# Layer 2 of a two-layer recurrent kernel: query and key norms together, keys kept in their bank, decay means moved to the tail, chunk sums in quarters

## The reference

```python
xn = layer_norm(x, ln1_w, ln1_b)
q, k, v = heads(xn @ Wq), heads(xn @ Wk), heads(xn @ Wv)
q = l2_normalize(q);  k = l2_normalize(k)
alpha = sigmoid(xn @ Wg + bg)
log_a   = log(maximum(alpha, 1e-6))
la_cum  = cumsum(log_a, within a chunk)
la_mean = la_cum.mean(-1)
decay   = exp(la_mean[:, None] - la_mean[None, :]) * tril
o_intra = ((q @ k.T) * decay) @ v
kv_chunk = (k * exp(la_cum[-1] - la_cum)).T @ v
chunk_decay = exp(log_a.sum())
q_dec = q * exp(la_cum)
# scan over the four chunks: o = q_dec @ S ; S = S * chunk_decay + kv_chunk
x = x + (o_intra + o_inter) @ Wo
x = x + gelu(layer_norm(x) @ W1 + b1) @ W2 + b2
```

## Time and profile before

| what | value |
|---|---|
| median of three executions | 2235.43 us (2231.66 to 2240.91) |
| the profiled execution, its own time | 2234.39 us |
| its span in the trace | 2232.6 us |
| TensorE busy | 1934.6 us, 87% |
| VectorE busy | 1362.9 us, 61% |
| ScalarE busy | 1096.1 us, 49% |
| mean granted TensorE clock | 0.953 of full |

### The profile page before, as it was taken

The page is one execution under the profiler, slowest core; times in us unless marked ns, Lnnn a source line. Parts: engine busy times, 40 slices in busy tenths (PEclk is TensorE's granted clock), DMA queues, the critical chain, the costliest instruction groups (busy, mean ns, idle before and its releaser), DMA issues.

```text
span 2232.6 us, 50773 instructions
## 1 busy us (share of the span) xinstructions
PE 1934.6 (87%) x17956; PEld 1381.8 (62%) x17972; DVE 1362.9 (61%) x3678; ACT 1096.1 (49%) x2434; POOL 214.6 (10%) x235
## 2 busy tenths in 40 slices
PE   6999999998999999959888988898988899898652
PEld 4666666666666666636667566765766676666552
DVE  6666666666666666637665765577666566755312
ACT  3444444443555445425665465555555554555332
POOL 0000000000000000030011001101111110010022
PEclk9999999999999999969999999999999999999887
DMA  3222222222122211230221112110211111111374
GB/s 127 79 87 87 87 87 92 91 86 64 59 68 68 67 49 53 75 116 23 63 67 47 56 56 66 52 30 24 67 46 58 58 53 41 37 46 42 124 233 119
DMA packets 97041, 159.05 MB, mean 71 GB/s; under 512 B 14279, under 2 KB 65607, under 8 KB 93640
## 3 DMA queue, kind: packets, MB, share of 16 engines
q1 hardware_dynamic: 87720, 134.93, 18.7%
q0 software_dynamic: 9248, 23.17, 3.4%
HBM read 96.35 MB, written 61.69 MB: 71 GB/s over the span
## 4 chain that ended last, share of the span: by engine, by line
PE 59%; DVE 20%; ACT 7%; issue 7%; SPq 3%; DMA 2%; POOL 1%; another core or an unknown queue 1%; DVEq 0%; ACTq 0%; POOLq 0%
PE psum L1032 5%; PE psum L870 5%; PE psum L937 4%; PE psum L830 4%; PE psum L764 3%; PE psum L1012 3%; PE psum L987 3%; PE psum L1142 3%; PE psum L952 2%; PE psum L1090 2%; PE psum L959 2%; PE psum L786 2%; PE psum L904 2%; PE psum L1041 2%; PE psum L877 2%
## 5 line engine op out<-in xcount | busy, mean ns | idle before, releaser
L1349 ACT ACTIVATE pts<-psum 128x512 f32<-128x512 f32 x192 | 99.1, 603 | 201.1 <-PE psum L904 201.1
L1803 DVE TENSOR_REDUCE mneg<-psum 128x2 f32<-128x512 f32 (+1 forms) x192 | 119.1, 683 | 46.8 <-PE psum L885 25.1
L671 POOL DMA_INDIRECT rows<-h,recA x64 | 61.5, 961 | 894.7 <-DVE recA L1585 767.3
L786 PE MATMUL psum<-txT,wt 128*128 128x128 f32 x864 | 118.9, 281 | 32.1 <-ACT txT L1241 32.0
L786 PEld LDWEIGHTS psum<-txT,wt 128*128 128x128 f32 x864 | 106.7, 194 | 43.9 <-ACT txT L1241 38.4
L870 PE MATMUL psum<-wa,xT_s 128*128 128x512 f32 x256 | 118.0, 603 | 2.6 <-DVE mneg L1803 2.6
L1032 PE MATMUL psum<-xT_s,wa 128*128 128x256 f32 x512 | 116.6, 381 | 0.0
L695 POOL DMA_INDIRECT rows<-xn,recC x32 | 31.5, 983 | 861.5 <-DVE recC L2007 741.3
L1550 DVE TENSOR_TENSOR tg<-tg,psum 128x256 f32<-128x256 f32 x84 | 35.2, 419 | 113.6 <-ACT tg L1230 109.2
L1032 PEld LDWEIGHTS psum<-xT_s,wa 128*128 128x128 f32 x512 | 95.8, 192 | 12.9 <-issue 1.0
L795 PE MATMUL psum<-wt,tg 128*128 128x128 f32 x528 | 79.2, 280 | 14.6 <-DVE tg L1552 13.8
(11 more groups left out here) (272 smaller groups left out, 4862.7 us busy)
## 6 DMA issues: line engine op xcount, KB each, us to landing
wt<-in_wB SPq DMA_DIRECT2D x84, 384.0 KB, 2.9
outs<-pbd SPq DMA_DIRECT2D x16, 1024.0 KB, 7.2
wt<-in_wD SPq DMA_DIRECT2D x24, 578.0 KB, 3.5
wa<-in_wD SPq DMA_DIRECT2D x15, 578.0 KB, 3.6
tx<-rows SPq DMA_DIRECT2D x132, 64.0 KB, 2.9
outs<-ty SPq DMA_DIRECT2D x132, 64.0 KB, 1.6
rows<-pbd SPq DMA_DIRECT2D x64, 128.0 KB, 1.7
rows<-pbd SPq DMA_DIRECT2D x8, 1024.0 KB, 3.9
```

Source lines behind the costliest of these rows:

```text
L786: last = mm(bank(f"th{j}")[:, c * P:(c + 1) * P], view[s][:, c * P:(c + 1) * P], txT[:, s, :], start=True, stop=True)
L1349: af(pT[:, n, :], bank(f"e{n}"), ACT.Exp, scale=float(HD) ** -0.5).then_inc(*frees(f"e{n}"))
L1803: ins = v.tensor_reduce(mneg[:, int(n >= 4), col:col + hs], sc, AX.X, ALU.max, negate=True)
```

## The change

Six edits, all in the P and C stages.

1. **Norms.** The squared queries and the squared keys are summed per head by a 128x32 matrix `headsum` into one bank `nq` (32 rows per group of four heads: queries in columns 0 to 255, keys in 256 to 511). One clamp, one logarithm and one exponential serve both. The query norms are spread to 64 rows by `headrow` (banks `rb`), the key norms are turned to token order (`rkT`).
2. **Keys.** The second projection of the keys is gone: `tk` is now 16 transposes of `kT`, and VectorE multiplies the decay with the bank directly. The copy, the squares in token order and their reduction go.
3. **Key projection.** `lk` moves from the tail of the previous turn to the head of C, between `te` and tile step 0.
4. **Decay means.** The logarithm (`decays`, ScalarE) and the means and their spreading (`decay_means`, VectorE) move from the head of C to the tail of the turn before; the clamps (L1686) move ahead of `wo1`. TensorE's first work in C is now `d`.
5. **Quarters.** `d`, `te` and `la` are computed in 64x64 pieces, one for each half of rows and half of columns. For that the second half of the heads has its two chunks swapped in `z` (`chunk_rows`).
6. **Bias of z.** `ones3` and `bg3` are kept in four row groups; the four bias products are issued together, ahead of the wait for the turned inputs. At the program's start that takes 4 loads of `ones3` in place of 1 and 12 small DMAs for `bg3` in place of 3, and ScalarE, VectorE and TensorE wait for 192 on `bg3_ready` in place of 48.

The core of the diff, SyncE's loads and TensorE:

```diff
+        def chunk_rows(half, ch):
+            r = ch ^ half
+            return slice(r * CH, (r + 1) * CH)
...
-            load(ones3[:, :], A["ones3"])
+            for g in range(4):
+                load(ones3[32 * g:32 * g + 3, :], A["ones3"])
...
             for i in range(3):
-                sp.dma_start(bg3[i:i + 1, :], kd_b16(i)).then_inc(sem("bg3_ready"), 16)
+                for g in range(4):
+                    sp.dma_start(bg3[32 * g + i:32 * g + i + 1, :], kd_b16(i)).then_inc(sem("bg3_ready"), 16)
...
-            def z_products(t):
+            def z_products():
+                places = [(t, c) for t in range(NT) for c in range(2)]
+                for g, (t, c) in enumerate(places):
+                    pe.wait_ge(*emptied(f"z{t}{c}"))
+                    mm(bank(f"z{t}{c}"), ones3[32 * g:32 * g + 3, :], bg3[32 * g:32 * g + 3, c * 512:(c + 1) * 512], start=True, stop=False)
+                pe.wait_ge(*read_out("zT"))
+                for t in range(NT):
+                    mm(bank(f"z{t}0"), xT[:, 1, t * P:(t + 1) * P], lqkvg[:, 3 * INNER:3 * INNER + 512], start=False, stop=True).then_inc(*fills(f"z{t}0"))
+                    pe.sem_inc(sem("tiles_open"), 1)
+                    for ch in range(2):
+                        place = chunk_rows(1, ch)
+                        last = mm(bank(f"z{t}1")[place, :], xT[:, 1, t * P + ch * CH:t * P + (ch + 1) * CH], lqkvg[:, 3 * INNER + 512:4 * INNER], start=False, stop=True)
+                    last.then_inc(*fills(f"z{t}1"))
...
             def attention1():
                 zT = xT[:, 1, :]
+                pe.wait_ge(*given("at3_ready", 0))
+                quads = [(hh, ch) for hh in range(2) for ch in range(2)]
+                for t in range(NT):
+                    for hh in range(2):
+                        pe.wait_ge(*emptied(f"d{t}{hh}"))
+                        mm(bank(f"d{t}{hh}"), identb[:, :], dmask[:, :, :], start=True, stop=False)
+                    pe.sem_inc(sem("tiles_open"), 1)
+                    for hh, ch in quads:
+                        rows = chunk_rows(hh, ch)
+                        last = mm(bank(f"d{t}{hh}")[ch * CH:(ch + 1) * CH, :], strict[rows, rows], at3[rows, t, 8 * hh:8 * hh + 8, :], start=False, stop=True)
...
+                    for hh, ch in quads:
+                        rows = chunk_rows(hh, ch)
+                        last = mm(bank(f"te{t}{hh}")[ch * CH:(ch + 1) * CH, :], strict[rows, rows], a_tok[rows, t, hh * 512:(hh + 1) * 512], start=True, stop=True)
...
+                products("lk", INNER)
+                tile_step(0)
                 pe.wait_ge(*given("sq_done", 0))
+                pe.wait_ge(*given("sk_done", 4))
                 for j in range(4):
-                    pe.wait_ge(*emptied(f"nq{j}"))
+                    pe.wait_ge(*read_out(f"lk{j}"))
+                pe.wait_ge(*emptied("nq"))
+                pe.sem_inc(sem("tiles_open"), 1)
+                for i, squares in enumerate((sqT, sqK)):
                     for a in range(2):
-                        last = mm(bank(f"nq{j}")[:, a * N:(a + 1) * N], samehead[:, :], sqT[:, 2 * j + a, :], start=True, stop=True)
-                    last.then_inc(*fills(f"nq{j}"))
-                for t in range(NT):
-                    for c in range(2):
-                        pe.wait_ge(*emptied(f"tk{t}{c}"))
-                        mm(bank(f"tk{t}{c}"), zT[:, t * P:(t + 1) * P], lqkvg[:, INNER + c * 512:INNER + (c + 1) * 512],
-                           start=True, stop=True).then_inc(*fills(f"tk{t}{c}"))
-                tile_step(0)
+                        for j in range(4):
+                            last = mm(bank("nq")[32 * j:32 * j + 32, i * N:(i + 1) * N], headsum[:, a, :], squares[:, 2 * j + a, :], start=(a == 0), stop=(a == 1))
+                last.then_inc(*fills("nq"))
                 tile_step(1)
...
+                for t in range(NT):
+                    last = tr(bank("rkT")[:, t * P:(t + 1) * P], rqk[:, 1, t * P:(t + 1) * P])
+                last.then_inc(*fills("rkT"))
+                for j in range(4):
+                    pe.wait_ge(*emptied(f"rb{j}"))
+                pe.sem_inc(sem("tiles_open"), 1)
+                for a in range(2):
+                    for j in range(4):
+                        rows = slice(32 * j, 32 * j + 32)
+                        last = mm(bank(f"rb{j}")[:, a * N:(a + 1) * N], headrow[rows, a, :], rqk[rows, 0, :], start=True, stop=True)
...
+                for t in range(NT):
+                    for c in range(2):
+                        pe.wait_ge(*emptied(f"tk{t}{c}"))
+                        for a in range(4):
+                            last = tr(bank(f"tk{t}{c}")[:, a * P:(a + 1) * P], kT[:, 4 * c + a, t * P:(t + 1) * P])
```

ScalarE at the head of C (after the decay exponentials), and VectorE's tail:

```diff
+                for j in range(4):
+                    act.wait_ge(*filled(f"lk{j}"))
+                    src = bank(f"lk{j}").rearrange("p (a n) -> p a n", a=2)
+                    af(sqK[:, 2 * j:2 * j + 2, :], src, ACT.Square).then_inc(*signals("sk_done"))
+                    af(kT[:, 2 * j:2 * j + 2, :], src, ACT.Copy).then_inc(*frees(f"lk{j}"))
+                tile_step(0)
+                first_gate()
+                act.wait_ge(*read_out("nq"))
+                af(rqk, rqk, ACT.Ln, scale=1e6).then_inc(*signals("act_chain"))
+                act.wait_ge(*chained("act_chain"))
+                af(rqk, rqk, ACT.Exp, scale=-0.5).then_inc(*signals("rq_ready"))
...
+                clamps()
                 dve.wait_ge(*filled("wo1"))
...
-                clamps()
+                decay_means(0)
+                decay_means(1)
                 tile_step(5)
```

235 lines of the change are left out of this document (114 added, 121 removed).

## The result

| | before | after |
|---|---|---|
| median, same chip | 2238.74 us (2231.66 to 2240.91, 6 runs) | 2255.92 us (2253.01 to 2265.38, 6 runs) |
| profiled execution | 2234.39 us | 2257.25 us |
| its span | 2232.6 us | 2255.5 us |
| TensorE busy | 1934.6 us | 1860.7 us |
| TensorE's matmul records | 17956 | 20500 |

The changed kernel takes 1.0089 times the time of before, 95% interval 1.0070 to 1.0108: 0.9% slower. 2200 us was forecast, and 2256 lies outside the range of 2150 to 2250.

What follows compares the result with a forecast made beforehand. TensorE's list was the main bound, VectorE holding it at certain places. B turns 33, D turns and CP 25, CD 0.6 gave -58.5; one-time costs +3.4 and +7, clock +13: net -35, 2200 us, range 2150 to 2250.

Steps and rivals of the forecast that it cites:

- Price of the quarters: Four 64x64 quarter products over 512 columns on TensorE were taken at 1.0 us, with ends of 0.86 and 3.5.
- Rival (a): Quarters of d and te run one behind the other, 3.5 us for 1.0: 2336 us, slower; chance 0.08.
- Change of tile shape: Eight more tiling switches a turn, taken as free; at 0.34 us each 44 in all, 2243 us.
- Head up to the scores: B turn's start: 1.5 us wait for the last key square, scores at 23.6 us, la following the scores to 28.2.
- The last state: VectorE's last chunk state ends 35.8 us into a turn: 1.8 us earlier in B turns, 0.6 in D turns.
- TensorE's work, per turn: Sum of TensorE's savings in norms, keys, d, te, la and z, less additions: 7.4 us less per turn.
- z: The z products fall from 5.4 to 3.6 us as bias products move into a wait: 1.8 us a turn.
- Tail: Turn's end: Gelu's table load 0.7 us earlier, behind two logarithms; decay means hidden; moving lk out costs nothing.
- Turns: Whole turns of layer 2: B turns of 66.9 us and D turns of 61.7.
- The clock: 3.5 us more at 1.2 GHz in every second turn, 0.45 each: 13 us added.
- Rival (b): Every turn has 6.8 us at 1.2 GHz: 49 us for 13, 2236 us; chance 0.15 together with the switches.
- Start: More DMAs and loads at the program's start: +7 us, ScalarE's first layer 1 work near 25 us for 18.48.

Runs made afterwards that it cites:

- n7: n5 with the key projection and ScalarE's squares and copies put first in C, ahead of d and te: 2198.11 us, ratio 0.9845.
- e1: The changed kernel with the cumulative decays (la) as 16 whole 128x128 products again, loops kept: 2223.79 us, ratio 0.9949.
- e4: The kernel before with 84 useless 64x64 products added to each turn of layer 2, nothing else: 2375.60 us, ratio 1.0606.
- n5: e1 with 49 more TensorE instructions (12 useless products, a semaphore step) run once ahead of layer 2's loops: 2228.52 us, ratio 0.9984.
- n9: e1 with 113 more TensorE instructions (28 useless products, a semaphore step) run once ahead of layer 2's loops: 2214.62 us, ratio 0.9916.
- n3: n1 with the key projection back in the tail and the keys' squares taken from SBUF in the head: 2280.75 us, ratio 1.0229.
- n1: The changed kernel with whole cumulative decays and TensorE's B loop written out, the D loop kept: 2208.94 us, ratio 0.9901.
- n10: n9 with the key projection and ScalarE's squares and copies put first in C: 2186.26 us, ratio 0.9785.
- e2: The changed kernel with TensorE's list written out for all turns of layer 2: 2218.10 us, ratio 0.9926.
- n6: e1 with 149 more TensorE instructions (37 useless products, a semaphore step) run once ahead of layer 2's loops: 2217.52 us, ratio 0.9919.
- n12: n10 with the first eight heads' decays in quarters again and 109 one-off instructions between the loops: 2164.37 us, ratio 0.9682.

## Why the prediction was wrong

The single turn `CPB` of the changed kernel, which has no branch ahead of it and the full clock, is the fairest test of the steps (its d begins at 1465.13):

```profile
1465.66 1.09 PE L1057 MATMUL psum<-reg,strict 64*64 64x512 f32 x8
1466.68 0.61 PE L1053 MATMUL psum<-dmask,identb 128*128 128x512 bf16 x2
...
1475.66 1.07 PE L1080 MATMUL psum<-reg,headsum 128*32 128x256 f32 x16 [1.88 <-ACT reg L1444]
...
1488.83 2.36 PE L1124 MATMUL psum<-qt,reg 64*64 64x64 f32 x128 [0.38 <-issue]
1490.99 1.71 PE L1139 MATMUL psum<-tri,big 64*64 64x64 f32 x102
1494.74 0.62 PE L1139 MATMUL psum<-tri,big 64*64 64x64 f32 x26 [2.03 <-issue]
...
1508.19 1.13 PE L839 MATMUL psum<-wa,xT_s 128*128 128x512 f32 x2
...
1512.32 3.84 PE L1195 MATMUL psum<-wa,pts 128*128 128x128 f32 x32
```

Even this turn took 68.75 us (1465.13 to 1533.89), 1.8 less than the same turn before the change (70.59), where 4.7 less was forecast.

- **Price of the quarters: right.** Four 64x512 products take 1.02 us (1466.68 - 1465.66); 1.0 was taken. Rival (a), a series of 3.5, is out. The Trainium skill, TensorEngine Tiling (Array Packing), Restrictions and Gotchas, says that different row tiles cannot access one PSUM bank at the same time; the rows don't bear it out where the two row halves write different partitions of the bank.
- **Change of tile shape: not free, as was taken, but far from 0.34.** Before, a mask product and the product behind it have one tile shape and start 0.21 us apart (first two rows below). In the changed kernel two mask products and the change to 64x64 take 0.53 (1465.66 - 1465.13), so the change costs 0.10 us. Eight more of them a turn would be some 13 us in all, an estimate from these rows.

```profile
1388.10 0.38 PE L1055 MATMUL psum<-dmask,identb 128*128 128x512 bf16 x1
1388.31 1.02 PE L1056 MATMUL psum<-reg,strict 128*128 128x512 f32 x2
```

- **Head up to the scores: right, in this turn.** The wait for the keys' squares ends 10.5 us in (8.5 to 10 forecast) after 1.88 us (1.5), the scores begin at 23.7 (23.6), la at 25.9 (by 26). In the looped B turn from 1392.57 they begin at 25.9 and 29.8, later than the 24 and 26 that the prediction named as a sign of being wrong. What was missed is that the wait need not be there: n7 took it away for 28 us.
- **The last state: wrong.** It was to end at 35.8 us; VectorE's last addition (L2028, 1502.03 and 0.69) ends at 37.6, as before the change. In the looped D turn from 1799.29 it ends at 38.4, for 36.4 before. The whole 1.8 us went into la, which took 4.4 us (1490.99 to 1495.4) where 2.4 stood, 2.03 of them issue.
- **This is the step that failed:** under "TensorE's work, per turn" the quarters were priced by their time on the array alone ("la 3.9 to 2.4"), and the growth of the list, from 1514 to 1853 instructions in a B turn, was put at nothing without a reason. 64 small products are 256 instructions, which have to be brought. In its place the runs showed 2.0 us of stall in la and 3.1 us and more of branch in each looped turn (e1, e4, n5 to n9), and the lower clock behind them.
- **z: smaller than forecast.** It takes 4.1 us where 3.6 to 3.9 was forecast. Each of its four products takes some 1.03 to 1.07 us (1508.19 to 1509.25), not the 0.9 of the earlier trace rows, and did so before the change too: four of them and four bias products made up the 5.4.
- **Tail: nearly right.** The table load stands right behind the two logarithms (1524.85 after 1522.79 and 2.04). TensorE's wait for the Gelu grew from 22.4 to 42.8 us, 1.3 us a turn, where 3.6 us of lk were taken out. n3, with lk back in the tail, waits 51.1 us and is 72 us slower than n1, so no run speaks against the nothing at which the move was costed.
- **Turns: wrong in the loops.** 66.9 and 61.7 were forecast; the trace has 72.6 to 76.9 and 64.7 to 66.9. No term and no rival held the branch.
- **The clock: too low.** 13 us were allowed, 29 came (105 us at the lower level for 41). In n9, where the branches are short, layer 2 has a clock of 0.97 and about 60 us at the lower level: some two thirds of the rise hung on the stalls. The mean of 0.95 in layer 2 is right at the bound that was named as a sign of being wrong. Rival (b) had the low heads right, and not their cause.
- **Start: right.** ScalarE's first work of layer 1 is at 24.47 us (25 forecast, 18.48 before). By the first turn of layer 2 the lag is 4.8 us (1013.58 for 1008.74), where 10.4 were taken for the start and GP.

58 us more of issue on TensorE (73 for 15: the branches, as far as they show as issue, and the dense runs) and 16 us of clock beyond the allowance are 74 us, for a miss of 56. The two sums can't be set against each other, since a stall can stand in place of a wait. With the same work, six D turns take 66.1 us each in n1, with branches of 3.3 us and more, and 64.9 in n9, with 0.2. Five B turns take 75.2 us each in e1 and 69.6 in n9; there the lower clock behind the branch comes on top.

The better test of the other terms is n9, whose loops fit and whose la is whole: a B turn, a D turn and fifteen turns.

```profile
1226.84:1294.83 67.99, 57.58 (x787) 43.70 (x787) 40.96 (x106) 37.66 (x79) 7.58 (x8) 1.00 0.20 62
1832.64:1897.49 64.85, 55.26 (x760) 41.88 (x761) 35.45 (x90) 32.52 (x70) 7.88 (x8) 0.97 0.16 50
1017.22:2027.19 1009.97, 855.98 (x11523) 639.32 (x11537) 572.85 (x1465) 520.04 (x1098) 107.72 (x114) 0.97 0.16 51
```

Without the 1.5 us for la that n9 doesn't have, the forecast's terms for these turns are -58 + 22 + 13 = -23 us; measured are 1009.97 - 1033.89 = -24. The B turn less 1.5 is 66.5 us for 66.9; the D turn less 1.5 and less 1.8 for its clock is 61.6 for 61.7. So the other terms were right in sum. Part of that is luck: z gave 1.3 us for 1.8 and the changes of tile shape were left out, while the clock cost less than the 13.

What stays open: why 7 blocks and not 8 hold; what a low stretch of 3.4 us that stays in the heads of n10 hangs on; and how much of the start's 5 us reaches the end.

## What to carry to other kernels

Splitting products into small tiles saves time on the array and spends instructions: count an engine's list per loop turn before and after such a change, and look whether its branch back and its instruction transfers change. Where a loop is near the limit, a shorter list (e1) or writing it out (e2) was worth 1.4 and 1.6% here, and a few useless instructions ahead of the loops, run once, decided over 11 to 15 us (n6 and n9 against n5). A wait that a change moves is as much worth looking at as the work it saves: here the order of the head (n7, n10) was worth 28 to 30 us, half of la in quarters (n12) 18.
